# Key scales per pair of groups, two-bank reads of key halves and another order of the first eleven steps in a graph attention kernel

## The reference

```python
h = jnp.maximum(_layernorm(x, axis=-1), 0.0)
q = h @ Wq.T + bq
k = key @ Wk.T + bk
v = value @ Wv.T + bv
adj_scores = (q @ k.T / 64) * adj_matrix
adj_scores = jnp.where(jnp.abs(adj_scores) < 1e-05, -1000000000.0, adj_scores)
prob = jax.nn.softmax(adj_scores, axis=-1)
out = x + (prob @ v) @ Wm.T + bm
```

## Time and profile before

| | us |
|---|---|
| median of three runs | 1617.06 |
| lowest and highest of them | 1616.17, 1618.53 |
| the profiled execution | 1620.5 |
| its span, first to last instruction | 1618.6 |
| PE busy in it | 1572.0 |
| DVE busy | 1006.6 |
| ACT busy | 606.8 |
| POOL busy | 95.8 |

### The profile page before, as it was taken

How to read it: one execution, slowest core, us unless ns; L and a number is a source line. 1 busy time by engine, 2 the same in 40 slices (tenths; PEclk the granted TensorE clock), 3 DMA queues, 4 the chain that set the end, 5 groups by cost and what they waited for, 6 DMA issues and landing times.

```text
span 1618.6 us, 23189 instructions
## 1 busy us (share of the span) xinstructions
PE 1572.0 (97%) x7180; PEld 715.8 (44%) x7180; DVE 1006.6 (62%) x2264; ACT 606.8 (37%) x975; POOL 95.8 (6%) x155
## 2 busy tenths in 40 slices
PE   8878899999999999999999999999999999999997
PEld 4443344444444444444444444444444444444442
DVE  4678756656666665666666666666666666666541
ACT  2666433333333333333333333333333333333331
POOL 0003200000000000000000000000000000000000
PEclk9998999999999999999999999999999999999999
DMA  9523465555555555554455555555555555555544
GB/s 350 215 65 72 111 137 118 130 118 123 128 118 123 132 121 122 122 131 117 118 134 123 125 121 118 130 121 119 136 117 126 124 127 119 118 132 125 120 101 78
DMA packets 431199, 205.72 MB, mean 127 GB/s; under 512 B 376128, under 2 KB 376128, under 8 KB 431040
## 3 DMA queue, kind: packets, MB, share of 16 engines
q1 hardware_dynamic: 430592, 205.07, 52.9%
q10 hardware_dynamic: 576, 0.27, 0.1%
...
## 4 chain that ended last, share of the span: by engine, by line
PE 91%; DVE 4%; ACT 2%; DMA 2%; issue 1%; SPq 0%; POOL 0%; DVEq 0%; ACTq 0%
PE O L467 13%; PE O L469 13%; PE O L468 13%; PE S L469 13%; PE S L468 13%; PE S L467 13%; PE M L467 3%; PE M L469 3%; PE M L468 3%; DMA pT<-ph 1%; DVE Zbuf L983 1%; DVE Zbuf L992 1%; ACT Vbuf L732 1%; PE O L532 1%; DVE Vbuf L1028 0%
## 5 line engine op out<-in xcount | busy, mean ns | idle before, releaser
L754 ACT ACTIVATE drop<-Zbuf 128x512 f32<-128x512 f32 x256 | 161.2, 630 | 795.8 <-DVE cmx L992 795.8
L983 DVE SCALAR_TENSOR_TENSOR Zbuf<-S,rs,adjb 128x512 f32<-128x512 f32 x256 | 192.0, 750 | 337.3 <-PE S L469 336.7
L467 PE MATMUL O<-Vbuf,pT 128*128 128x512 f16 x1024 | 388.2, 379 | 5.8 <-DMA pT<-ph 4.3
L467 PE MATMUL S<-Kbuf,qT 128*128 128x512 f16 x1024 | 389.6, 380 | 0.7 <-DMA qT<-row 0.7
L469 PE MATMUL S<-Kbuf,qT 128*128 128x512 f16 x1024 | 389.6, 380 | 0.0
L468 PE MATMUL S<-Kbuf,qT 128*128 128x512 f16 x1024 | 389.5, 380 | 0.0
L469 PE MATMUL O<-Vbuf,pT 128*128 128x512 f16 x1024 | 388.1, 379 | 0.0
L468 PE MATMUL O<-Vbuf,pT 128*128 128x512 f16 x1024 | 388.1, 379 | 0.0
L992 DVE CUSTOM_DVE_ANT_0 Zbuf<-drop,Zbuf 128x512 f32<-128x512 f32 x256 | 175.8, 687 | 0.0
L1017 DVE TENSOR_SCALAR drop<-drop,rs 128x512 f32<-128x512 f32 x256 | 143.8, 562 | 35.4 <-ACT drop L754 35.2
L467 PEld LDWEIGHTS O<-Vbuf,pT 128*128 128x128 f16 x1024 | 100.2, 98 | 130.4 <-DMA pT<-ph 7.7
...
## 6 DMA issues: line engine op xcount, KB each, us to landing
adjb<-in_adj_dram SPq DMA_DIRECT2D x256, 256.0 KB, 2.8
...
pT<-ph SPq DMA_TRANSPOSE x132, 3.1
...
```

Source lines behind the costliest of these rows:

```text
L467: nc.tensor.matmul(ps, lhs[0], rhs[0], start=start, stop=False)
L754: nc.scalar.activation(drop[:, :], Zbuf[:, s.p, s.c * CW:(s.c + 1) * CW], ACT.Abs).then_inc(abs_ready, 1)
L983: nc.vector.scalar_tensor_tensor(out=z, in0=S[s.j % 2][:, :], scalar=rs[:, r, 3:4], in1=adjb[:, s.j % ADJ_SLOTS, :], op0=ALU.add, op1=ALU. ...
```

## The change

All of it lies in the part ahead of step 0 and in the first eleven steps, except for two things that reach into the loop.

- **Key scales.** Each pair of key groups (0 and 1, 2 and 3, 4 and 5, 6 and 7) gets a scale of its own (`key_scales`, `largest_keys`; columns of `kst`). The pairs K0 and K1 are handled ahead of step 0, K2 and K3 in steps 0 to 3. All eight groups are squared on ACT. In the loop, `rs` and `unit` have four columns and an instruction takes the column of its pair; the row maximum is taken per pair, multiplied by the pair's unit and then reduced, five small operations for three.
- **Two banks at once.** Four banks lie side by side in one tensor R. From group 2 on ACT and DVE read two of them in one instruction of 1024 columns (`high_of_pair`, `low_of_pair`), the halves of B and the copies of Wm^T likewise.
- **Order.** Key loads come directly behind the weights, Wm, Wv and the values later. PE transposes key group 0 while A's scale is made, then projects q. Wm is transposed in step 2, the output bias is made in step 5, B in four rounds in steps 6 to 9 (a round adds one quarter of the inner dimension to all four parts), B's halves in step 10. The largest values of Wm and Wv are taken by DVE in steps 5 and 6, one scale chain serves them and the values in steps 7 and 8. Value tiles are scaled in steps 9 to 16, and tile 3 goes to POOL too. In block 0 the preparation of the next block's h and q stands one step later (`pc`). The first block's units are made by POOL (`first_row_units`).

```diff
         S = [bank("S0"), bank("S1")]
-        W = [bank("W0"), bank("W1")]
-        O = [bank("O0"), bank("O1")]
-        M0, M1 = bank("M0"), bank("M1")
+        R = ctx.enter_context(nc.psum_tensor("R", [P, 4, 512], fp32))
+        W, O, M0 = [R[:, 0, :], bank("W1")], [R[:, 1, :], R[:, 2, :]], R[:, 3, :]
+        M1 = bank("M1")
...
-        FILLS = ["A"] * ND + ["Wm^T"] * ND + ["B"] * (ND - 1) + [0] * ND + ["B"] + [1] * ND + ["bias"]
+        FILLS = ["A"] * ND
+        for g in range(NC):
+            FILLS += ["Wm^T"] * ND * (g == 5) + [g] * ND
+        FILLS += ["bias"] + ["B"] * ND
+        RING = [W[0], O[0], O[1], M0]
...
-        V_SQUARES = [1, 2, 3, 4, 5, 6, 8, 10]
-        V_TILES = [0] * 8 + [4 * n for n in range(9)]
-        V_FIRST = V_TILES.count(0) - 1
+        V_SQUARES = [0, 0, 0, 0, 1, 3, 6, 10]
+        V_TILES = [0] * 10 + [4 * n for n in range(1, 9)]
...
+        WM_STEP, BIAS_STEP, B_STEPS, B_OUT = 2, 5, {6: 0, 7: 1, 8: 2, 9: 3}, 10
+        VB_LARGEST, VB_SCALES = 7, 8
+        V_LOADS = [(1, 2), (3, 4), (5, 6), (7, 8, 9)]
...
-            return j % 4 == 3 and j > 3
+            return j % 4 == 3
...
+            def key_high(g):
+                act.wait_ge(k_small, 4 * (g // 2 + 1))
+                act.wait_ge(start_mm, last_fill(g) + 1)
+                if g < FIRST_KEYS:
+                    for s in range(ND):
+                        high_of(k_pair(g, 0, s), kst[:, 4, g // 2:g // 2 + 1])
+                else:
+                    for s in range(0, ND, 2):
+                        high_of_pair(k_pair(g, 0, s, 2), kst[:, 4, g // 2:g // 2 + 1])
...
+            def low_of_pair(high, low, scale):
+
+                nonlocal fill
+                dve.wait_ge(start_hi, sum(f not in ("Wm^T", "bias") for f in FILLS[:fill + 2]))
+                nc.vector.scalar_tensor_tensor(out=low, in0=pair_of_banks(fill), scalar=scale, in1=high,
+                                               op0=ALU.mult, op1=ALU.subtract).then_inc(start_dve, 2)
+                fill += 2
...
-                        nc.vector.tensor_reduce(smx[:, q, 0:1], cmx[:, q, :], X, ALU.max).then_inc(rowmax_ready, 1)
+                        nc.vector.tensor_reduce(smx[:, q, 0:NPAIR], cmx[:, q, :].rearrange("p (a b) -> p a b", b=2), X, ALU.max)\
+                            .then_inc(rowmax_ready, 1)
                         wait(dve, exp_done, NPAIR * (s.b - 2))
-                        nc.vector.tensor_copy(smx[:, q, 2:3], unit[:, q:q + 1]).then_inc(smax_ready, 1)
-                        wait(dve, rowmax_ready, s.b)
-                        nc.vector.tensor_scalar(smx[:, q, 1:2], smx[:, q, 0:1], unit[:, q:q + 1], -1.0,
-                                                ALU.mult, ALU.mult).then_inc(smax_ready, 1)
+                        nc.vector.tensor_copy(smx[:, q, NPAIR:2 * NPAIR], unit[:, q, :]).then_inc(smax_ready, 1)
+                        wait(dve, rowmax_ready, 3 * s.b - 2)
+                        nc.vector.tensor_tensor(smx[:, q, 0:NPAIR], smx[:, q, 0:NPAIR], unit[:, q, :], ALU.mult).then_inc(rowmax_ready, 1)
+                        wait(dve, rowmax_ready, 3 * s.b - 1)
+                        nc.vector.tensor_reduce(smx[:, q, 2 * NPAIR:2 * NPAIR + 1], smx[:, q, 0:NPAIR], X, ALU.max).then_inc(rowmax_ready, 1)
+                        wait(dve, rowmax_ready, 3 * s.b)
+                        nc.vector.tensor_scalar(smx[:, q, 2 * NPAIR + 1:2 * NPAIR + 2], smx[:, q, 2 * NPAIR:2 * NPAIR + 1], -1.0, None,
+                                                ALU.mult).then_inc(smax_ready, 1)
```

675 lines of the change are left out of this document (407 added, 268 removed).

## The result

The changed kernel took 1606.81 us in the median of 4 runs (1605.86 to 1607.24), beside 1617.80 for the kernel before, run on the same chip (4 runs, 1616.17 to 1619.35). The ratio is 0.9930, its 95% interval 0.9918 to 0.9942: 11.0 us or 0.7% faster. The forecast was 1600.5, inside 1588 to 1612.

A forecast was written before the change was run, and what follows sets the result against it. PE's own work bounds the loop, DVE with ACT the first 18 steps. First pass 24.9 us earlier, 20.1 left at step 9, 16.5 at step 19's projection: 1617.06 - 16.5 = 1600.5 us, range 1588 to 1612.

The forecast's parts named there:

- my forecast: Whole kernel: the central case, 1594 to 1606 us around 1600.5, given chance 0.51.
- rival (b): Steps before the loop: slow PE bursts after waits and POOL locks leave less gain, 1606 to 1613 us; chance 0.20.
- that start: PE's start of step 19's q projection, at 191.61 us after its last wait, for `ho`; forecast 16.5 us earlier.
- Up to the first pass: Kernel start to step 0's pass on DVE (one pass per step): 46.5 us for 71.40, 24.9 earlier.
- The read of two banks: DVE, steps 0 to 8: 1024 elements take 1.26 us for the 1.41 of two reads, saving 1.8.
- the idle time of steps 0 to 8: DVE between the passes of steps 0 and 9: waits placed queue by queue, 11.9 us together.
- DVE with ACT, not PE, sets the pace of the first 18 steps: Premise for steps 0 to 17: DVE with its partner ACT is the bound, so times are summed along DVE.
- SP's queue, in step 3: Bound in step 3: `ho`'s transpose behind three value loads may hold DVE, part of a 7 us gain, 1610.
- from the pass of step 18 to PE's last wait: DVE's pass of step 18 to PE's projection of step 19: 6.7 us, carried over from before.
- rival (c): Steps with value tiles: POOL's tiles delay PE's value products, gain given back whole, within 0.2%; chance 0.05.
- (a): Start of the kernel: PE, not DVE, is the floor and idle time nearly all goes, 1586 to 1594; chance 0.17.
- (d): Loop: row maximum's five dependent operations delay each block, making it slower, 1631 at 1 us per block; chance 0.07.

The follow-up runs named there:

- experiment 4: Changed kernel with the first pair of key groups scaled by the largest of all eight squares: 1620.56 us, ratio 1.0019 to the kernel before.
- experiment 6: Changed kernel with the transpose into `ho` issued first by SP in steps 3 and 18, and value tile 31 split by DVE, not POOL: 1599.45 us.
- experiment 1: Changed kernel with every read of two banks (1024 columns) made as two reads of 512, same place and order: 1607.93 us.
- experiment 9: Changed kernel with the transpose into `ho` issued first in step 18 only, and value tile 31 split by DVE instead of POOL: 1600.75 us.
- experiment 3: Changed kernel with step 2's transposes of Wm ahead of that step's key transposes: 1607.48 us.
- experiment 8: Changed kernel with `ho` transpose first in steps 3 and 18, Wm ahead of keys in step 2, POOL on the third value tile of four: 1607.81 us.
- experiment 5: Changed kernel with SP issuing the transpose into `ho` first in steps 3 and 18, ahead of adjacency tile, value loads and probabilities: 1603.03 us.
- experiment 10: Changed kernel with the transpose into `ho` issued first in step 3 only: 1603.87 us.
- experiment 2: Changed kernel with the last value tile (31) split by DVE instead of POOL, nothing else: 1605.53 us.
- experiment 11: Changed kernel with six more dependent multiplications by one in the row maximum of every block: 1608.51 us.

## Why the prediction held, and where it was off

**How far it held.** The time lies in the stated range, 1588 to 1612, but above the 1594 to 1606 that I called my forecast, in the part that the range took in for rival (b). Of the 16.5 us forecast 11.0 came (13.4 between the two spans). The start was right, and what the steps give back was put too low.

**The method.** "Whatever brings that start forward by x brings the end forward by x" held. In experiment 4 the first pass moved by 14.8 us, PE's last wait by 14.7 and the time by 13.8. In experiment 6 the projection moved by 6.6 and the time by 7.4.

**Up to the first pass.** 24.9 us forecast, 24.5 measured. The chain was right in its parts too: `ho`'s low half ended at 28.2 (27.9), the row scales at 39.1 (39.0), the first score stood at 44.02 (43.5). Experiment 4 splits the 24.5: at most 14.8 are the scale that no longer needs all eight groups, at least 9.7 the work that left the start.

**The read of two banks.** 1.26 forecast, 1.27 measured for one alone; the saving of 1.8 is 1.4 in DVE's busy time, and some 0.4 of it reaches pass 9 (experiment 1). The busy time of DVE was right within 1.2 us in both stretches.

**The step that failed: the idle time of steps 0 to 8.** I had 11.9 "placed by going through the queues step by step", and it was 17.2. The waits that I placed were there and of the right size but for two (3.3 for 1.9 in step 3, 2.5 for 1.8 in step 0); what was missing are the waits for ACT's key highs in the other steps, 2.4 in all, and some tenths more. Part of the 3.3 is PE at the lower clock in Wm's transposes (3.36 us for the 2.33 of experiment 9, behind the same wait). But removing that wait gave nothing (experiments 3 and 8), and issuing `ho` early gave 1.9 at pass 8 (experiments 5 and 10). So the largest wait in the list was not the one that counted. Behind this stands a premise that failed. The prediction says that DVE with ACT, not PE, sets the pace of the first 18 steps, and sums along DVE. From 77.48 to 118.60 it is PE: busy 41.12 of 41.12 us, with DVE at 31.07. What counts there is when this stretch of PE's can begin, and that hung on `ho`: 1.9 us earlier at the projection are 1.9 at pass 8 (experiments 5 and 10), 1.8 later are 2.0 (experiment 1), while Wm's place changed nothing (8, beside 5). `ho` behind three value loads was named in the bounds ("SP's queue, in step 3"), where it made part of the time of 1610, and had no term in the sum.

**The second step that failed: from the pass of step 18 to PE's last wait.** I carried over the 6.7 us of before. But PE's last wait was another one, for POOL's tile 31, at the value product of step 18. Against rival (c) I had written that "after them 3 us and more are free before the projection of step 19". They are not free: the wait for POOL was 3.52 and the slow product behind it 1.7. One tile later than before, with the statistics of the next block ahead of it in POOL's queue, the value tiles became the deadline in step 18 only. This is rival (c)'s mechanism at one of its eight places. Experiments 2, 6 and 9 show it with its partner, `ho` behind the probabilities: tile 31 gives 1.3 us by itself and 3.6 where `ho` is first (experiments 5 and 6); `ho` in step 18 gives 0.8 by itself (experiments 10 and 5) and 4.8 where tile 31 is DVE's (2 and 9); both together 6.1. The 1.3 and the 0.8 are not resolved by these medians.

**The account of the miss.** The result is 6.3 us above 1600.5. The projection is 6.0 late; from there 2.9 were gained; the step from the profiled execution to the median cost 2.3, as the forecast took the difference of two profiles off a median, and the profile of before stood 2.3 us further above its median than that of after does; and the median of before that stood beside it was 0.7 higher than the one shown first. Together 6.1. So the sum in the trace's own time was off by 3.1, of a gain of 13.4 between the spans, and 3.0 are the base and the measurement.

**The rivals.** (a), PE as the floor: its mechanism is true of steps 4 to 9, its price is not, as I had looked only for the idle time that would go, not for the busy time that stays; my argument against it, that DVE's own work leaves no room, was wrong there. (b), 1606 to 1613, is where the time fell. Its mechanism, slow bursts and locks, has a share: the product of 4.27 us at 171.67 is one such burst on the path, and POOL's lock is there at every tile, 4.8 us in all, but before had 4.4 of them too, so the eighth tile added 0.4 for the 0.5 of the sum. The one of 1.05 us at 173.26 cost nothing, as DVE waits for PE right after (2.66 at the pass of step 19). (c) is answered above. (d), the loop: six operations more per block, three times the two that the change added (it made five of three; what I wrote before experiment 11 says of two, which leaves out the copy), cost 1.7 us by the medians and 1.0 between the traces, where 34 would be the full price. The cover stands.

**Left open.** In which part the profiled execution of before was slower than its median. Whether PE runs slowly behind a wait of a given length can't be told from these runs (below). And how much of the first pass's gain needs the scale per pair, with PE's queue in another order.
